# The inverse roots of the gated stage as one power on GpSimd

## The reference

```python
qkv = (x @ qkv_w + qkv_b).reshape(B, N, 3, H, HD)     # H = 12 heads, HD = 64
q, k, v = qkv[0], qkv[1], qkv[2]                      # after a transpose
q = _layernorm(q, q_norm_w, q_norm_b)                 # (x - m) * rsqrt(v + 1e-5) * w + b
k = _layernorm(k, k_norm_w, k_norm_b)
attn = softmax((q * scale) @ k.T)
o = masked_gates[..., None] * (attn @ v)
return o @ proj_w + proj_b
```

## Time and profile before

| | |
|---|---|
| median of three runs | 567.08 us (565.38 to 567.10) |
| the profiled execution, its own time | 564.13 us |
| its span, first to last instruction | 562.3 us |
| TensorE (PE) busy | 515.8 us, 92% |
| VectorE (DVE) busy | 405.9 us, 72% |
| ScalarE (ACT) busy | 299.1 us, 53% |
| GpSimd (POOL) busy | 88.8 us, 16% |
| mean granted clock of TensorE | 0.991 of full speed |

### The profile page before, as it was taken

One profiled execution on the slowest core, in us unless ns is written; L12 is line 12 of the kernel. 1 busy time (PEld: TensorE's weight loads), 2 busy tenths in 40 slices (PEclk: granted clock), 3 DMA queues, 4 the chain that ended last, 5 costly groups with the idle time before them and its releaser, 6 DMA issues. The chain is left out here.

```text
span 562.3 us, 11393 instructions
## 1 busy us (share of the span) xinstructions
PE 515.8 (92%) x4691; PEld 395.9 (70%) x4691; DVE 405.9 (72%) x891; ACT 299.1 (53%) x489; POOL 88.8 (16%) x70
## 2 busy tenths in 40 slices
PE   7999989879999899999999899899968898989696
PEld 6766568659877567787967668677945777775475
DVE  5325877898777866969677866869648688747982
ACT  1153454673286547767266447766246467525762
POOL 1042200002122242010011333000100311011200
PEclk9999999999999999999999999999979999999999
DMA  9993020000000001000000000000000000000000
GB/s 283 271 218 104 1 64 1 8 2 1 1 2 2 2 1 56 7 3 2 1 24 1 2 2 1 0 2 0 2 23 1 2 1 1 1 22 1 1 2 21
DMA packets 13443, 16.02 MB, mean 28 GB/s; under 512 B 6491, under 2 KB 10960, under 8 KB 13008
## 3 DMA queue, kind: packets, MB, share of 16 engines
q1 hardware_dynamic: 9712, 12.71, 8.6%
q10 hardware_dynamic: 3680, 2.59, 1.6%
HBM read 14.11 MB, written 1.18 MB: 27 GB/s over the span
## 5 line engine op out<-in xcount | busy, mean ns | idle before, releaser
L1733 DVE TENSOR_REDUCE smax<-ps 96x12 f32<-96x1152 f32 (+1 forms) x28 | 37.8, 1349 | 17.1 <-PE ps L1063 9.9
L1747 DVE TENSOR_REDUCE psum<-pr 128x12 f32<-128x1152 f32 (+1 forms) x24 | 32.3, 1345 | 5.0 <-ACT pr L1386 4.9
L1381 ACT ACTIVATE pr<-ps,less 128x96 f32<-128x96 f32 (+1 forms) x96 | 24.6, 337 | 18.3 <-DVE less L1735 18.2
L1424 ACT ACTIVATE squares<-ps 128x1536 f32<-128x1536 f32 x12 | 17.4, 1450 | 28.4 <-PE ps L705 20.9
L1846 DVE TENSOR_REDUCE ss<-squares 128x24 f32<-128x1536 f32 x12 | 21.0, 1749 | 13.5 <-ACT squares L1424 13.4
L1975 POOL TENSOR_TENSOR side_wide<-attn,w_mask 128x1024 f32<-128x1024 f32 (+1 forms) x12 | 20.7, 1748 | 59.1 <-ACT attn L1276 47.4
L2001 POOL TENSOR_TENSOR squares<-squares,qk_root 128x512 f32<-128x512 f32 x8 | 16.6, 2081 | 75.6 <-DVE qk_root L1516 75.6
L685 PE MATMUL ps<-w_cqkv,side_c 64*96 64x384 f32 (+1 forms) x96 | 27.4, 500 | 0.0
L1949 POOL TENSOR_TENSOR ln_root<-ln_root,minus_half 128x3 f32<-128x3 f32 x8 | 6.9, 856 | 127.3 <-DVE ln_root L1621 127.3
L695 PE MATMUL ps<-w_cqkv,side_c 128*128 128x512 f32 (+1 forms) x72 | 26.2, 510 | 0.0
L1012 PE MATMUL ps<-w_ff,b_kB 128*128 128x192 f32 x144 | 25.5, 329 | 0.0
(11 more groups left out here) (364 smaller groups left out, 1337.7 us busy)
## 6 DMA issues: line engine op xcount, KB each, us to landing
x_in<-in_xT SPq DMA_DIRECT2D x3, 768.0 KB, 4.4
b_kB<-in_cqkv SPq DMA_DIRECT2D x1, 1152.0 KB
w_cqkv<-in_cqkv SPq DMA_DIRECT2D x1, 864.0 KB
out<-side_c ACTq DMA_DIRECT2D x3, 288.0 KB, 2.3
w_cqkv<-in_cqkv SPq DMA_DIRECT2D x1, 855.0 KB
heads<-in_xT ACTq DMA_DIRECT2D x3, 256.0 KB, 4.4
side_in<-in_patchT SPq DMA_DIRECT2D x3, 192.0 KB, 3.9
side_tok<-in_tok_ff SPq DMA_DIRECT2D x2, 288.0 KB, 5.8
```

What stands on the lines that cost most here:

```text
L1381: m = act.activation(e[:, s % 2, h * N:(h + 1) * N], t[0:rows, h // 4, h % 4 * N:(h % 4 + 1) * N], ACT.Exp, scale=head ** -0.5, bias=less[ ...
L1424: act.activation(sq.rearrange("p (b n) -> p b n", b=3), t[:, :, :], ACT.Square).then_inc(w.S["sq"], 1)
L1733: dve.tensor_reduce(mx, t, AX.X, ALU.max).then_inc(w.S[stage + "_sub"], 1)
L1747: dve.tensor_reduce(psum[0:rows, s % 2, :], e, AX.X, ALU.add).then_inc(w.S[done], 1)
```

## The change

The ten steps and the function `inverse_root` go. VectorE writes the variance (one instruction) and waits; GpSimd raises all 24 columns to the power -0.5 in one instruction; VectorE then scales all 24 heads. GpSimd scales no heads any more, and the semaphore that told of it (`qkn`) goes, with the wait for the tile before (`pooled_before`). The constant `minus_half` is widened from 6 to 24 columns. The transposes wait for VectorE's scale alone.

```diff
-ROOT_SEED, ROOT_SCALE = 0x5F3759DF, 64.0 / 9.0
-ROOT_STEPS, POWER_STEPS = 10, 2
-DVE_HEADS = 16
+POWER_STEPS = 2
...
-        minus_half = sb("minus_half", [128, 2 * TILES_B])
+        minus_half = sb("minus_half", [128, 2 * NH])
...
             def c_qt(w, tile):
-                pe.wait_ge(w.S["qkn"], w.upto("qkn", w.c, tile + 1))
-                pe.wait_ge(w.S["qk_root"], w.upto("qk_root", w.c, (tile + 1) * (ROOT_STEPS + 1)))
+                pe.wait_ge(w.S["qk_root"], w.upto("qk_root", w.c, 3 * tile + 3))
...
             def c_qk(w, tile):
                 dve.wait_ge(w.S["sq"], w.upto("sq", w.c, tile + 1))
                 dve.tensor_reduce(ss[:, :], sq.rearrange("p (h d) -> p h d", d=HD2), AX.X, ALU.add)\
                    .then_inc(w.S["ss"], 1)
                 dve.wait_ge(w.S["ss"], w.upto("ss", w.c, tile + 1))
-                if tile > 0 or w.c > 0 or w.chain == "e":
-                    dve.wait_ge(*pooled_before(w, tile))
-                inverse_root(w, qk_root, 2 * NH, "qk_root", w.c, tile * (ROOT_STEPS + 1),
-                             lambda: dve.tensor_scalar(qk_root[:, 0, :], ss[:, :], ROOT_SCALE / HD2, ROOT_SCALE * EPS,
-                                                       ALU.mult, ALU.add))
+                powered(w, "qk_root", w.c, 3 * tile, [
+                    lambda: dve.tensor_scalar(qk_root[:, 0, :], ss[:, :], 1.0 / HD2, EPS, ALU.mult, ALU.add)])
                 dve.wait_ge(w.S["qk_raw"], w.upto("qk_raw", w.c, tile + 1))
                 qk = qkn[tile % 2].rearrange("p (h d) -> p h d", d=HD2)
-                qk = qk[:, 0:DVE_HEADS]
-                dve.tensor_tensor(qk, qk, qk_root[:, 1, 0:DVE_HEADS].unsqueeze(2).to_broadcast([128, DVE_HEADS, HD2]), ALU.mult)\
+                dve.tensor_tensor(qk, qk, qk_root[:, 1, :].unsqueeze(2).to_broadcast([128, 2 * NH, HD2]), ALU.mult)\
                    .then_inc(w.S["qk_root"], 1)
...
             def c_qk(w, tile):
-                pool.wait_ge(w.S["qk_root"], w.upto("qk_root", w.c, tile * (ROOT_STEPS + 1) + ROOT_STEPS))
-                pool.wait_ge(w.S["qk_raw"], w.upto("qk_raw", w.c, tile + 1))
-                qk = qkn[tile % 2].rearrange("p (h d) -> p h d", d=HD2)[:, DVE_HEADS:2 * NH]
-                pool.tensor_tensor(qk, qk, qk_root[:, 1, DVE_HEADS:2 * NH].unsqueeze(2)
-                                   .to_broadcast([128, 2 * NH - DVE_HEADS, HD2]), ALU.mult).then_inc(w.S["qkn"], 1)
+                power(w, qk_root, 2 * NH, "qk_root", w.c, 3 * tile + 1)
```

More of the change, by code:

```diff
@@ L223 @@
 PER_C = {
-    "c_T": 2, "h2b": 1, "g_step": 23, "g_exp": 1, "gates": 2, "sq": 3, "qk_raw": 3, "ss": 3, "qk_root": 3 * (ROOT_STEPS + 1),
-    "qkn": 3,
+    "c_T": 2, "h2b": 1, "g_step": 23, "g_exp": 1, "gates": 2, "sq": 3, "qk_raw": 3, "ss": 3, "qk_root": 9,
     "c_qkT": 3, "c_v": 4, "c_mid": 4, "c_sub": 12, "c_exp": 8, "c_pT": 4, "c_w": 16, "c_oT": 4, "out_tm": 3, "out_dma": 16,
@@ L1495, in powered @@
                 dve.wait_ge(w.S[name], w.upto(name, group, done + len(starts) + 1))
[L1497 to L1516, removed]
             def a_en(w, _):
@@ L1834, in c_g @@
                 assert step[0] == PER_GROUP["g_step"], step[0]
[L1836 to L1842, removed]
             def c_qk(w, tile):
```

## The result

The changed kernel took 590.58 us (median of four runs, 589.88 to 595.03), the kernel before 566.23 us (563.79 to 567.10; three of its four runs are those shown ahead). The ratio is 1.046, with a 95% interval of 1.042 to 1.050: **slower by about 26 us**, 0.0463 x 566.2, with 24 to 28 us as the interval; the two medians alone lie 24.35 us apart. The forecast was 596.5 us, 29.4 more than the median shown ahead of it, and the range was 582 to 606.

What follows compares the result with a forecast made beforehand. TensorE, busy 92%, was taken to set the pace, with VectorE moving the end in the last group. 564.13 + 23.35 of late handovers + 6 of clock = 593.5 us, as a median 596.5; range 582 to 606.

Steps and rivals of the forecast that it cites:

- The power's price: GpSimd's power on 24 columns: 4.17 us, by a straight line through two, three and six columns.
- both rivals on it: Power cheap on many columns, 566 or 564.5 us, chance 0.05; column price falls beyond six, 577 us, chance 0.05.
- Scale, hold and lead: Per tile: VectorE's scale 1.76 us; variance start to scale end 6.23, 2.86 more; variance start to transposes 6.28, 1.95 more.
- The handovers: Variance end to power start 0.08 us, power end to VectorE 0.04, and 0.05 on to TensorE.
- The walk: VectorE's order followed through four groups for uncovered delay: 5.2, 4.85, 4.7 and 8.6 us, sum 23.35.
- What was costed at nothing: First group's third tile, GpSimd's own queue and the removed wait for the tile before: no cost expected.
- The clock: TensorE falls to half clock after the new waits; four falls not hidden, 0 to 3.4 us each: 6 us taken.
- From the sum to the time: Profiled execution's 564.13 us + 23.35 + 6 = 593.5, scaled in proportion to a median of 596.5.
- the third rival: Power line holds, but the clock stays up or later waits take some back: 582 to 591 us, chance 0.16.

Runs made afterwards that it cites:

- kernel with six columns: Changed kernel with the power on 6 columns instead of 24, whose roots scale all 24 heads: 563.73 us, ratio 0.9988.
- kernel with shorter fillings: Changed kernel with TensorE's seven longest waits filled by unread identity products, fewer than in a first try: 586.44 us, ratio 1.0381.
- kernel with the later scale: Changed kernel with each tile's scale a separate step later in VectorE's order, and two buffers for sums and roots: 573.59 us, ratio 1.0163.
- kernel with the third scale put off: From the kernel with the later scale, the third tile's scale in the first two groups moved behind the first two samples' largest scores and sums: 576.78 us, ratio 1.0205.
- that with 12 columns: Changed kernel with the power on 12 columns instead of 24, roots repeated to scale all heads: 572.05 us, ratio 1.0128.
- the ten steps with all heads: Kernel before, keeping the ten steps, but VectorE scales all 24 heads and GpSimd none: 566.05 us, ratio 1.0028.
- the last group alone: The change in the last group's three tiles only; other groups keep the ten steps and shared scale: 572.75 us, ratio 1.0155.

## Why the prediction was right, and where it was off

- **The power's price.** 4.17 us forecast by a line through three points, 4.17 measured. The price doesn't stop growing at six columns, nor does it fall: both rivals on it are out, and 12 columns lie on the line too.
- **Scale, hold and lead.** 1.76, 6.23 and 6.28 us forecast; 1.76, 6.22 and 6.28 measured. The handovers, taken from a layer norm, held.
- **The walk.** First to last group 5.2, 4.85, 4.7 and 8.6 forecast; 5.0, 4.7, 4.7 and 8.25 measured, 22.7 instead of 23.35. The largest part, the last group, is confirmed by a run of its own (ratio 1.0155).
- **What was costed at nothing.** The third tile of the first group: the step behind it on VectorE (line 1540 after) began at 233.63, 10.3 us later than in the earlier trace rows, and TensorE's start on x2T had been 10.2 later; it cost 0.1. GpSimd's queue, the removed wait and the new semaphores cost nothing that can be measured, as the kernel with six columns shows.
- **The clock.** This is the term that was mis-sized: 6 us forecast, some 3 in the profiled executions, 4.1 to 4.6 by the times with their wide intervals. The falls that the change made were five, between the two and six that I named as bounds, but I counted four that are not hidden. The first was: the slow transposes used up the wait before x2T, which was 1.48 us and not 3.2. That of 547 to 554 ran out in front of the next wait, the one of 4.47 us until 560.17. Three are left. In the second group TensorE's first product on x2T took 2.21 us instead of 1.46, in the third and the last group the last transposes 2.79 instead of 1.50. Against the kernel with shorter fillings, 0.5 us were lost from the second group's stretch to the third's, 1.9 from the third's to the last's, and 0.3 behind the last.
- **From the sum to the time.** I counted 29.4 us on 567.08. Measured are 26.2 by the ratio and 25.7 in the profiled executions from the first variance on. Of the 3 to 4 us between, the clock has nearly 3, and the walk about 1 (23.35 forecast, 22.45 by the kernel with shorter fillings). The kernel before also came out 0.85 us lower with its fourth run than in the three I started from.
- **Against its own range.** 590.6 us lies just below the forecast's own 592 to 602 and inside the third rival's 582 to 591, near its top; in that rival later waits take back some of the loss. Mechanism and prices were those of the forecast; in how much of the clock is hidden, the rival was nearer. The 6 us of clock was a choice between 0 and 13 and not worked out fall by fall. That the wide range holds the time is owed to the walk, which is nearly nine tenths of the loss.

It was not tried whether the power can be cheaper on another engine, and no kernel here beats the kernel before by more than can be measured.

## What to carry to other kernels

A chain of many tiny instructions that looks wasteful can be shorter than the one that replaces it: ten steps of 0.2 us on the engine that needs the result against 4.2 us on another, with nothing to do in between. Price the new instruction at its real width before the move, from the same kernel where it can be had, and then ask what stands behind the waiting instruction in its engine's queue, group by group; the step that frees the engine (here the scale put off) gave back two thirds of the loss, while busy time told nothing of it. A wait of TensorE can carry a second price, its clock (it fell after waits of 2.99 to 5.78 us here), of which only that part counts that no later wait hides.

## What the runs showed of the hardware

**A power that starts beside a VectorE product takes longer.** In the kernel with the later scale, powers that began 0.17 us after VectorE's scale took 5.60 us, at 213.37 and in the second group at 347.99, instead of 4.17: 1.43 more, close to the 1.58 us that the scale still had to run. The kernel with the third scale put off shows it twice more (5.60 us). The other way round nothing was seen: in the last group the scale began at 530.41, just after the second power had begun (526.20 + 4.14 = 530.34), and took 1.78 us, and three powers took 12.43 us together, 4.14 each. The Trainium skill, SBUF — State Buffer, in the section "SBUF: two separate sides", says that VectorE and GpSimd share a port pair as an exclusive lock, for VectorE instructions of certain modes or, against a GpSimd instruction that reads SBUF, with two inputs in SBUF as this scale has; the one that starts first holds the pair for its whole instruction while the other blocks. The first pair of rows agrees with it; the second, where the scale began behind the power and was not held up, does not.

**The power is priced by the column.** 0.38 us and 0.158 us for each column of 128 values, from 2 to 24 columns.

**The same steps keep the full clock in one execution and lose it in another.** Ahead of the first variance all kernels here run the same steps. One product there, in the kernel before and then in the kernel after:

```profile
105.94 2.25 PE L1063 MATMUL ps<-b_kB,heads 32*32 32x192 f32 x96 [1.36 <-DVE b_kB L1723]
```

```profile
109.52 2.90 PE L1060 MATMUL ps<-b_kB,heads 32*32 32x192 f32 x96 [1.36 <-DVE b_kB L1698]
```

The wait ahead of it is the same, 1.36 us. In the kernel before the granted clock stayed at 1.00; in the kernel after it was 0.50 from 112 to 116, as it had been from 16 to 20. Traces without such a fall in this part (the kernel before, that with 12 columns, the ten steps with all heads, the last group alone, the shorter fillings) reach the first variance at 204.7 to 205.4 us, those with one at 205.9 to 206.8, and those with two at 208.3 to 210.55. So falls of the clock go with some 5 us of difference in the same steps, and a difference of that size between two profiled executions is read only from the first changed instruction on.
